# The end of an expert loop: last round added through PSUM, closing sums in the same block

## What is computed

```python
scores = softmax(x @ gate_w.T); topk_w, topk_ids = top_k(scores, 4)   # 32 experts, 4 per token
buf[e, pos] = x[tok]                    # rows sorted by expert, at most C per expert, others dropped
gu = einsum('ech,ehf->ecf', buf, w13)   # 512 -> 2 x 256
act = silu(g) * u
eo = einsum('eci,eih->ech', act, w2)    # 256 -> 512
out_slots = eo[sorted_eid, pos]         # a row beyond C reads what the index gives, the last slot
routed = zeros.at[tok].add(out_slots * flat_w)
out = residual + routed + shared
```

## Time and profile before

| | us |
|---|---|
| median of 3 runs | 1285.64 |
| lowest, highest | 1282.01, 1287.48 |
| profiled execution | 1286.82 |
| its span in the trace | 1285.0 |
| first closing DMA is issued | 1247.8 |
| first scatter of the expert loop | 816.1 |

### The profile page before, as it was taken

One profiled execution on the slowest core, in us unless ns is written; L12 is line 12 of the kernel. 1 busy time (PEld: TensorE's weight loads), 2 busy tenths in 40 slices (PEclk: granted clock), 3 DMA queues, 4 the chain that ended last, 5 costly groups with the idle time before them and its releaser, 6 DMA issues. The chain is left out here.

```text
span 1285.0 us, 21982 instructions
## 1 busy us (share of the span) xinstructions
PE 1093.1 (85%) x6180; PEld 826.6 (64%) x6198; DVE 854.9 (67%) x1561; ACT 523.9 (41%) x1092; POOL 417.1 (32%) x327
## 2 busy tenths in 40 slices
PE   6999799788887759887859996999999999999842
PEld 6989666434443428777847764777777777777630
DVE  3547449878875628888756895767677676766415
ACT  1332152366674258677524242433333333333210
POOL 0000001111110201666733001456566556655420
PEclk8999899999999788888768999999999999999975
DMA  7323500100000486534063312878789898777539
GB/s 276 135 98 155 204 25 1 17 1 0 0 1 1 154 287 224 199 145 181 1 248 145 71 56 82 238 182 231 187 235 233 203 234 224 200 191 176 81 63 378
DMA packets 100284, 185.19 MB, mean 144 GB/s; under 512 B 13737, under 2 KB 32425, under 8 KB 100240
## 3 DMA queue, kind: packets, MB, share of 16 engines
q1 hardware_dynamic: 79856, 141.33, 32.6%
q0 software_dynamic: 18080, 38.85, 15.6%
q10 hardware_dynamic: 2304, 4.46, 0.9%
HBM read 138.50 MB, written 50.86 MB: 147 GB/s over the span
## 5 line engine op out<-in xcount | busy, mean ns | idle before, releaser
L2235 POOL DMA_INDIRECT y_d<-tail,x_ox x80 | 169.0, 2112 | 135.6 <-ACT tail L2400 110.1
L1536 POOL DMA_INDIRECT x_g<-r_d,x_ix x82 | 87.2, 1063 | 138.6 <-issue 115.6
L2293 PE MATMUL x_h<-x_w_hi,x_t_hi 128*128 x320 | 128.1, 400 | 2.2 <-DVE x_t_lo L2416 2.2
L2294 PE MATMUL x_h<-x_w_lo,x_t_hi 128*128 x320 | 127.7, 399 | 0.0
L2295 PE MATMUL x_h<-x_w_hi,x_t_lo 128*128 x320 | 127.7, 399 | 0.0
L210 POOL TENSOR_TENSOR ln_rstd<-ln_ve,powers 128x2 f32<-128x2 f32 (+1 forms) x40 | 26.2, 655 | 265.5 <-DVE ln_ve L204 265.5
L2416 DVE TENSOR_TENSOR x_w_lo<-w,x_w_hi (+1 forms) x64 | 109.6, 1753 | 2.6 <-ACT x_w_hi L2374 2.6
L2365 ACT ACTIVATE x_gs<-x_h 128x256 f32<-128x256 f32 x80 | 30.7, 385 | 187.5 <-PE x_h L2295 172.4
L2416 DVE TENSOR_TENSOR x_t_lo<-x_xb,x_t_hi 128x512 fp32r<-128x512 f32 x80 | 55.3, 692 | 43.0 <-ACT x_t_hi L2360 42.8
L1268 ACT ACTIVATE h_d<-h_negm,h_g 128x256 f32<-128x256 f32 x128 | 63.7, 498 | 28.6 <-DVE h_negm L1440 26.8
L2312 PE MATMUL x_o<-x_w_hi,x_avt_hi 128*128 x160 | 72.0, 450 | 1.5 <-issue 1.1
(11 more groups left out here) (371 smaller groups left out, 2671.8 us busy)
## 6 DMA issues: line engine op xcount, KB each, us to landing
w<-in_L_ffn_w SPq DMA_DIRECT2D x32, 1024.0 KB, 8.6
h_negm<-negm_d SPq DMA_DIRECT2D x16, 1024.0 KB, 7.1
w<-in_L_ffn_w SPq DMA_DIRECT2D x32, 512.0 KB, 10.0
raw<-in_L_ffn_w SPq DMA_DIRECT2D x3, 2816.0 KB, 16.8
x_res<-in_x SPq DMA_DIRECT2D x8, 512.0 KB, 4.9
ctx_in<-in_ctx SPq DMA_DIRECT2D x8, 512.0 KB, 3.5
kt_d<-ct SPq DMA_DIRECT2D x8, 512.0 KB, 3.1
vc_d<-ctx_in SPq DMA_DIRECT2D x8, 512.0 KB, 2.6
```

What stands on the lines that cost most here:

```text
L1536: nc.gpsimd.indirect_dma_start(out=xg[q][s][:], out_offset=None, in_=r_d, in_offset=bass.IndirectOffsetOnAxis(ap=ix[q][:, s:s + 1], axis=0 ...
L2235: nc.gpsimd.indirect_dma_start(out=y_d[s], out_offset=bass.IndirectOffsetOnAxis(ap=ox[q][:, s:s + 1], axis=0), in_=eo[q][s][:], in_offset= ...
L2293: nc.tensor.matmul(hbank[s][:], hi[:, k, :], w13p[0][:, at, k, :], start=k == 0, stop=False)
L2294: nc.tensor.matmul(hbank[s][:], hi[:, k, :], w13p[1][:, at, k, :], start=False, stop=False)
```

## The change

It has four parts.

1. The two last rounds no longer begin with a wait for all scatters. In round 2n ACT waits for the scatters of the rounds before only where it writes `eo`, DVE where it writes `ox`. Gathers that nobody uses are left out of round 2n.
2. Round 2n + 1 scatters nothing. ACT casts its result banks to high parts and DVE forms low parts (into the buffers `xt`, `eop`). DVE builds one-hot matrices of its 256 slots (`hot`, `hot_early`, `hot_last`), and PE multiplies them with the high and low parts, so that each of the 16 row tiles gets its added rows in PSUM, 4 matmuls per tile, and then the shared rows' product (`add_lost`). The slot numbers are made ready by `last_slots` on DVE between round 1 and the hardware loop, part of the one-hots by `one_hots_early` between the loop and round 2n.
3. The closing block is gone; its loads, sums and stores stand at the end of each engine's program in the loop's block. They begin when the scatters of round 2n have landed and the last silu is done (`rows_done`). The tables are loaded into `w13p[1]` and `x` instead of tiles of their own, all on SP's queue, in pieces of 1 MB; the shared rows in eight pieces of 64 KB on ACT's queue. There are 8 chunks of 2 row tiles.
4. The PSUM tiles of the loop are cut from four double banks, and one 64 KB load (`count_row`) is added to SP's queue in the routing stage.

```diff
@@ gpsimd
-            round_of(2 * n, 0)
-            round_of(2 * n + 1, 1, more=False)
+            round_of(2 * n, 0, more=False)
             for s in range(2):
-                pool.wait_ge(added[s], 32 * n + 32)
+                pool.wait_ge(added[s], 32 * n + 16)
+            pool.wait_ge(gs_ready, 4 * n + 4)
+            pool.sem_inc(rows_done, 1)
@@ sync
+            sp.wait_ge(rows_done, 1)
+            for c in range(CH // 2):
+                for h in range(2):
+                    sp.dma_start(parts[h][:, 2 * R * c:2 * R * (c + 1), :],
+                                 token_rows(y_d[h][0:T, :], 2 * R * c, 2 * R)).then_inc(part_in[c], 16)
+            for c in range(CH):
+                sp.wait_ge(summed, c + 1)
+                sp.dma_start(token_rows(out.rearrange("b s d -> (b s) d"), R * c, R),
+                             parts[0][:, c * R:(c + 1) * R, :]).then_inc(stored, 16)
+            sp.wait_ge(stored, 16 * CH)
@@ tensor
+            def add_slots(c, s):
+                for t in range(c * R, (c + 1) * R):
+                    rows = hot_early[:, t, :] if s == 0 and t < EARLY else hot[s][:, t, :]
+                    nc.tensor.matmul(tile_of(t), rows, eop[s][0], start=s == 0, stop=False)
+                    nc.tensor.matmul(tile_of(t), rows, eop[s][1], start=False, stop=False)
+            def add_lost(c):
+                for t in range(c * R, (c + 1) * R):
+                    g = t % 4 * NE
+                    last = nc.tensor.matmul(tile_of(t), lost_t[g:g + NE, t // 4, :], final[g:g + NE, 0, :],
+                                            start=False, stop=True)
+                last.then_inc(tile_ps, 1)
+            pe.wait_ge(hot_ready, 1)
+            pe.wait_ge(eo_lo, 1)
+            for c in range(3):
+                add_slots(c, 0)
+            pe.wait_ge(eo_lo, 2)
+            ...                                  # 4 matmuls with hot_last into last_bank
+            pe.wait_ge(hot_ready, 2)
+            for c in range(3):
+                add_slots(c, 1)
+            pe.wait_ge(final_ready, 1)
+            for c in range(3):
+                add_lost(c)
+            pe.wait_ge(hot_ready, 4)
+            for c in range(3, CH):
+                if c >= 4:
+                    pe.wait_ge(summed, c - 3)
+                for s in range(2):
+                    add_slots(c, s)
+                add_lost(c)
@@ scalar
                 for s in range(2):
                     act.wait_ge(eo_ps, OPEN + 2 * i + s + 1)
+                    if not more:
+                        nc.scalar.copy(eop[s][0], obank[s]).then_inc(eo_hi, 1)
+                        continue
-            for s in range(2):
-                act.wait_ge(added[s], 32 * n)
-            round_of(2 * n, 0)
+            round_of(2 * n, 0, before=2 * n)
             round_of(2 * n + 1, 1, more=False)
+            act.wait_ge(rows_done, 1)
+            for h in range(2):
+                for g in range(4):
+                    act.dma_start(final[g * NE:(g + 1) * NE, h], y_d[h][T + P:, :]).then_inc(final_in, 16)
@@ vector
             round_of(1, 1)
+            last_slots()
             with dve.Fori(0, n - 1) as i:
                 ...
+            one_hots_early()
+            round_of(2 * n, 0, before=2 * n, ahead=False)
+            round_of(2 * n + 1, 1, more=False, ahead=False)
             for s in range(2):
-                dve.wait_ge(added[s], 32 * n)
-            round_of(2 * n, 0)
-            round_of(2 * n + 1, 1, more=False)
+                dve.wait_ge(eo_hi, s + 1)
+                lo_part(eop[s][1], obank[s], eop[s][0]).then_inc(eo_lo, 1)
+            one_hot(hot[1][:, 0:EARLY], 1, 0, EARLY).then_inc(hot_ready, 1)
+            one_hot(hot[1][:, EARLY:], 1, EARLY, NT).then_inc(hot_ready, 1)
+            one_hot(hot[0][:, EARLY:], 0, EARLY, NT).then_inc(hot_ready, 1)
+            dve.wait_ge(final_in, 128)
+            steps.then(nc.vector.tensor_tensor(final[:, 0], final[:, 0], final[:, 1], ALU.add))
+            dve.wait_ge(tile_ps, 1)
+            nc.vector.tensor_tensor(final[:, 0], final[:, 0], last_bank, ALU.add).then_inc(final_ready, 1)
             for c in range(CH):
+                mine, other = (parts[h][:, c * R:(c + 1) * R, :] for h in range(2))
+                dve.wait_ge(part_in[c // 2], 32)
+                steps.then(nc.vector.tensor_tensor(mine, mine, other, ALU.add))
+                dve.wait_ge(tile_ps, c + 2)
+                nc.vector.tensor_tensor(mine, mine, banks[c % 4][:], ALU.add).then_inc(summed, 1)
```

More of the change, by code:

```diff
@@ L2292, in up @@
                 for k in range(KD):
[L2293 to L2295 removed]
+                    nc.tensor.matmul(hbank[s], hi[:, k, :], w13p[0][:, at, k, :], start=k == 0, stop=False)
+                    nc.tensor.matmul(hbank[s], hi[:, k, :], w13p[1][:, at, k, :], start=False, stop=False)
+                    last = nc.tensor.matmul(hbank[s], lo[:, k, :], w13p[0][:, at, k, :], start=False, stop=k == KD - 1)
                 last.then_inc(h_ps, 1)
@@ L2317, in down @@
                 for f in range(KI):
-                    last = nc.tensor.matmul(obank[s][:], lo[:, f, :], w2p[0][:, at, f, :], start=False, stop=f == KI - 1)
+                    last = nc.tensor.matmul(obank[s], lo[:, f, :], w2p[0][:, at, f, :], start=False, stop=f == KI - 1)
                 last.then_inc(eo_ps, 1)
@@ L2350, in _, with tile_of @@
             rest(n, 1, experts_of(2 * n + 1))
+            def tile_of(t):
+                return banks[t // 2 % 4][:, t % 2]
+            def add_slots(c, s):
[15 more added lines that the diff above has]
+            for s in range(2):
+                for p in range(2):
+                    last = nc.tensor.matmul(last_bank, hot_last[s][:].rearrange("p g e -> p (g e)"), eop[s][p],
+                                            start=s + p == 0, stop=s + p == 2)
+            last.then_inc(tile_ps, 1)
+            pe.wait_ge(hot_ready, 2)
[8 more added lines that the diff above has]
+                    pe.wait_ge(summed, c - 3)
+                for s in range(2):
+                    add_slots(c, s)
+                add_lost(c)
         @block.scalar
@@ L2464, in scatter_rows, with round_of @@
                 nc.vector.tensor_copy(ox[q][:], route[:, 0, ds(2 * r, 2)]).then_inc(ox_ready, 1)
-            def round_of(r, q, more=True, before=None, opening=False):
+            def round_of(r, q, more=True, before=None, opening=False, ahead=True):
                 codes_next = [code_of(dve, 2 * r + 1), code_of(dve, 2 * r + 2)] if more else None
-                if more:
+                if ahead:
                     gather_rows(r + 2, q)
@@ L2478, in round_of @@
                     turned(r + 1, 1)
+                if not more:
+                    return
                 scatter_rows(r, q, before)
@@ L2500, in _ @@
                 round_of(2 * i + 3, 1, before=2 * i + 2)
+            one_hots_early()
+            round_of(2 * n, 0, before=2 * n, ahead=False)
+            round_of(2 * n + 1, 1, more=False, ahead=False)
             for s in range(2):
-                dve.wait_ge(added[s], 32 * n)
-            round_of(2 * n, 0)
-            round_of(2 * n + 1, 1, more=False)
[L2507 to L2525, removed]
-            for c in range(CH):
[L2527 to L2553, removed]
-            dve.wait_ge(final_in, 32 * R)
-            nc.vector.tensor_tensor(final[:, 0], final[:, 0], final[:, 1], ALU.add).then_inc(final_ready, 1)
-            for c in range(CH):
-                mine, other = (parts[:, h, c * R:(c + 1) * R, :] for h in range(2))
-                dve.wait_ge(part_in[c], 32)
-                nc.vector.tensor_tensor(mine, mine, other, ALU.add).then_inc(paired, 1)
-                dve.wait_ge(paired, c + 1)
-                dve.wait_ge(lost_ps, c + 1)
-                nc.vector.tensor_tensor(mine, mine, lost_y[c % 2][:], ALU.add).then_inc(summed, 1)
```

68 lines of the change are left out of this document (54 added, 14 removed).

## The result

| | before | changed |
|---|---|---|
| median, first chip | 1285.39 us (4 runs) | 1273.69 us (4 runs, 1269.92 to 1276.60) |
| ratio, first chip | | 0.9903, 95% interval 0.9883 to 0.9923 |
| median, second chip | 1286.27 us (11 runs) | 1269.06 us (5 runs, 1266.35 to 1272.88) |
| ratio, second chip | | 0.9871, 95% interval 0.9849 to 0.9894 |
| span of the profiled execution | 1285.0 us | 1274.8 us (first chip), 1267.5 us (second) |

It is faster by 1.0 to 1.3%. The forecast was 1269 us, a ratio of 0.987, with a range from 1264 to 1277.

What follows compares the result with a forecast made beforehand. DMA engines were taken to bound the last 37.2 us. Span 1285.0 - 16.1 (earlier start) - 0.7 (shorter transfer) = 1268.2; with 1.82 around it 1270.0, less 1.18 for the median 1268.8, stated as 1269; range 1264 to 1277.

Steps and rivals of the forecast that it cites:

- Part 1, 6.3 us: Wait ahead of round 2n removed: gain of 4.87 us TensorE idle time and 1.44 us slow clock, 6.3 us taken.
- `last_slots`, 2.9 us: Start of the hardware loop: eight small DVE instructions and later reading of codes delay the loop 2.9 us, bounds 0 to 3.6.
- Start of the closing part, 16.1 us: First closing table load: issued at 1231.7 instead of 1247.80, 16.1 us earlier.
- 8.6 for the round: Closing loads wait for the scatter issued at 1230.36 in place of that at 1238.96: 8.6 us earlier.
- 3.7 for the block: No block end and new block start ahead of the closing loads: 3.7 us saved.
- The closing transfer, 36.5 us: From first closing load to the end: DMA-bound transfer takes 36.5 us against 37.2 before, bounds 35 and 39.
- (b): Closing part: TensorE at 1.2 GHz bounds the end, time 1280 us; chance 0.08.
- (c): Closing loads: one queue runs slower than two, 327 to 340 GB/s, 3.7 us more, time 1273; chance 0.05.
- (a): Closing part: shared rows come late behind table pieces, time 1272 us, or 1280 if served after all tables; chance 0.10.
- (e): Hardware loop: moved code makes each branch pass fetch instructions, 18 passes at 2.6 us are 47 us, time 1316; chance 0.03.
- (d): Closing loads: rows_done released no earlier than the last round's end, so the early start fails, time 1278.5; chance 0.03.

Runs made afterwards that it cites:

- the two experiments: Waits for all scatters ahead of round 2n put back into the changed kernel, ratio 0.9956; the same waits alone moved in the kernel before, ratio 0.9946.
- e10_two_queues: Changed kernel with two small shared-row loads on SP's queue ahead of the tables, and table y_d[1] loaded by ACT's queue; ratio to the kernel before 0.9873.
- e1: Changed kernel with the eight 64 KB shared-row loads on SP's queue ahead of the tables instead of on ACT's; ratio to the kernel before 0.9906.
- e2_warm_tensore: Changed kernel with 22 more matmuls, result unused, on TensorE just ahead of its wait for the shared rows; ratio to the kernel before 0.9892.
- e0: The changed kernel itself run again without edits, on the second chip; ratio to the kernel before 0.9871.
- e3: Changed kernel with last_slots moved from ahead of the hardware loop to the very start of VectorE's program in the block; ratio to the kernel before 0.9874.
- e4: Changed kernel with the two waits for all scatters put back ahead of round 2n, on ACT and VectorE; ratio to the kernel before 0.9956.

## Why the prediction came out as it did

**Part 1, 6.3 us.** Right, in place and size: 6.4, and 6.5 to 6.9, in the two experiments.

**`last_slots`, 2.9 us.** The mechanism was right, the term too small. I had 1.5 us for the instructions (it is 1.5) and 1.46 for the codes (1.86), and forgot what the idle time then does to TensorE's clock (0.6), which I had counted in part 1. It measures 4.0 us, and 3.1 to 3.9 in the other pairs that differ in its place alone; the bound of 3.6 was too low.

**Start of the closing part, 16.1 us.** 16.0 and 15.6 in the two traces, by the middle part. The shares came out too: with the wait moved alone 438.9, from there to the changed kernel's 429.7 it is 9.2, and with the 4.0 of `last_slots` given back 13.2. I had 8.6 for the round and 3.7 for the block, 12.3, and 0.4 of scatter distance. No run has the round or the block's end alone, so 13.2 holds both. That the sum came out to 0.5 us is part luck: a cost taken 1.1 too small and gains taken 0.6 too small make up for each other.

**The closing transfer, 36.5 us.** This is the step that failed: 41.6 and 38.7. It had 1237.8 for the landing of the shared rows, from eight issues of 0.44 us and 2.6 us to landing, and took that landing time from a row in which only small loads ran; the last landed at 1245.4. Beside the tables it is 6.6. ACT's issues also start 1.4 us after SP's, behind its last cast, and take 0.51 us each. From that followed an idle TensorE, for which I had allowed "a microsecond or two", and the slow clock of rival (b). The mixture itself also moved fewer bytes per us, which none of my cases held; (c) had a lower rate, but from the single queue. 41.6 is beyond the upper bound of 39. As the length of an undisturbed transfer 36.5 was near: 36.7 to 37.5 are reached once the small loads are few and out of the way.

**The rivals.** (a) and (b) had 0.10 and 0.08 as single cases; they come together, since the one makes the other's idle time. The rule that the prediction set beside (a), from the Trainium skill, "DMA: Bandwidth & Descriptors", section "Queues, rings and completion order" (each engine takes turns between queues), agrees in that the small loads were not held back until the tables were through: the last landed at 1245.4, before the last table load was issued at 1246.67. It led me to "within a few us" without a price; here each load landed 4.0 to 4.6 us later than in company of its own kind. The issues, which (a) feared for, were not blocked (0.51 us each). (c) and (e) are refuted, by e10_two_queues and by the middle part, which shrank. (d) did not happen: the first table load is issued at 1233.22.

**The total.** A span of 1274.8 and one of 1267.5 stand on both sides of the forecast's 1268.2. On the first chip the first column was 1.4 us later than before and the closing part 5.1 longer than forecast; on the second it was 3.3 us earlier and the closing part 2.2 longer. That the second median is at 1269 is thus part luck, and the first, 1273.69, lies in the range because that had been drawn to hold most of (a).

## What to carry to other kernels

Price a small load in the company it will have: load as few of the bytes that a chain waits for as can be, and these ahead of the bulk on the same queue. Eight loads moved ahead gained nothing that a run shows. When a wait is moved or added, count TensorE's clock with it: here 3.4 us of idle time cost 4.0. Small work with waits of its own is hidden where its engine waits for another anyway; look for such a gap in the trace, and check the time ahead of the first mark as well as behind it. And compare rates over stretches that begin at the same point of the work: the first 2 us of the table loads are slow in every trace here.

## What the runs showed of the hardware that was not expected

A 64 KB load into 32 partitions took 2.0 us from issue to landing among others of its kind (e1) and 6.6 us beside 1 MB loads of another queue. With both kinds under way the DMA share was 1.07 while the rate was 286 GB/s, against 387 at a share of 1.05 later. A part of this the small loads bring with them. Window of e1_shared_rows_first in which they run alone:

```profile
1234.00:1237.00 3.00, 3.00 (x15) 2.46 (x14) 3.00 (x4) 0.00 (x0) 0.00 (x0) 1.00 0.44 109
```

109 GB/s at a share of 0.44 are 248 at a full share, where the tables have 369. By this estimate the 0.52 MB of the eight loads cost 0.7 us more than as many bytes of a table; the rest of the lost rate, and the reason for either, are open.

The granted clock fell to 0.50, the lower of the two levels, after idle times of 5.6, 3.4 and 2.24 us and after one of 1.26 us with small matmuls and 0.78 us behind it. It held at 1.00 through 1.25 us in e2_warm_tensore, where full-size matmuls had run up to it. After work had begun again in the closing part it came back after 3 us in e1, 6 us in e0 and e3, and 12 us in the changed kernel's first trace and in e4. The last four are the same closing code, and TensorE was busy all the while; what decides between these was not tried.
